# Relative values in a bank of the transposes' ring, and all values of a tile in one run, two steps behind its scores

## What is computed

```python
scores = einsum('bhqd,bhkd->bhqk', Q, K) / SCALE
rel_k = pek[idx]                       # idx = clip(k - q, -256, 256) + 256
scores = scores + einsum('bhqd,qkd->bhqk', Q, rel_k) / SCALE
attn = softmax(where(causal, scores, -inf), axis=-1)
out = einsum('bhqk,bhkd->bhqd', attn, V)
rel_v = pev[idx]
out = out + einsum('bhqk,qkd->bhqd', attn, rel_v)
```

## Time and profile before

| | |
|---|---|
| median of 3 runs | 5531.92 us (5531.32 to 5532.51) |
| the profiled execution | 5535.59 us |
| its span in the profile | 5533.9 us |
| TensorE busy, share of the span | 93% |
| VectorE, ScalarE, GpSimd | 68%, 62%, 33% |
| DMA queue of SP, share of 16 engines | 77.5% |
| mean granted clock of TensorE | 0.990 |

### The profile page before, as it was taken

The page is one execution under the profiler, slowest core; times in us unless marked ns, Lnnn a source line. Parts: engine busy times, 40 slices in busy tenths (PEclk is TensorE's granted clock), DMA queues, the critical chain, the costliest instruction groups (busy, mean ns, idle before and its releaser), DMA issues. The chain is left out here.

```text
span 5533.9 us, 143122 instructions
## 1 busy us (share of the span) xinstructions
PE 5134.9 (93%) x49460; PEld 3347.5 (60%) x49460; DVE 3774.5 (68%) x8777; ACT 3425.3 (62%) x7512; POOL 1831.3 (33%) x2516
## 2 busy tenths in 40 slices
PE   9986999999999999999999999999999799999999
PEld 5554666666666666666666666666666455665665
DVE  5555777777777777777777777777777455555554
ACT  4445888878778887887877878778787211111111
POOL 3443333333333333333333333333333011111111
PEclk9997999999999999999999999999999899999999
DMA  7888999999999999999999999999999311111110
GB/s 223 254 252 264 329 323 324 332 316 323 321 324 324 325 323 321 324 328 325 322 325 327 322 321 327 316 323 327 324 322 304 99 61 56 50 61 61 61 55 32
DMA packets 654368, 1418.07 MB, mean 256 GB/s; under 512 B 64072, under 2 KB 362544, under 8 KB 641456
## 3 DMA queue, kind: packets, MB, share of 16 engines
q1 hardware_dynamic: 653744, 1409.89, 77.5%
HBM read 737.46 MB, written 672.14 MB: 255 GB/s over the span
## 5 line engine op out<-in xcount | busy, mean ns | idle before, releaser
L809 ACT ACTIVATE a_prob<-a_neg_s,a_neg_max 128x384 f32<-128x384 f32 (+1 forms) x1792 | 1081.1, 603 | 209.1 <-DVE a_neg_max L858 193.2
L524 DVE COPY a_p_t<-a_t_ps 128x512 f32<-128x512 f32 (+3 forms) x1536 | 952.5, 620 | 24.8 <-PE a_t_ps L773 23.9
L773 PE MATMUL a_t_ps<-a_ident,a_prob 128*128 128x128 f32 x5120 | 924.5, 280 | 31.5 <-DVE a_p_t L524 20.4
L858 DVE CUSTOM_DVE_ANT_1 a_neg_s<-a_s_ps,a_bias,a_far_neg 128x384 f32<-128x384 f32 x1280 | 791.0, 618 | 237.6 <-DVE a_far_neg L852 237.6
L706 PE MATMUL a_s_ps<-a_k,a_q 96*128 96x512 bf16 (+3 forms) x3072 | 852.7, 332 | 107.2 <-ACT a_far L813 105.1
L852 DVE TENSOR_REDUCE a_far_neg<-a_s_ps 128x1 f32<-128x640 f32 (+4 forms) x1280 | 708.8, 554 | 312.0 <-PE a_s_ps L706 178.5
L816 ACT ACTIVATE a_b_out<-a_t_ps 128x512 f32<-128x512 f32 (+1 forms) x1024 | 587.4, 574 | 384.4 <-PE a_t_ps L716 364.6
L734 PE MATMUL a_o_ps<-a_p_t,a_v 128*32 128x128 f32 x18432 | 782.0, 279 | 7.8 <-ACT a_o_t L821 0.2
L813 ACT ACTIVATE a_far<-a_s_ps,a_neg_max 128x640 f32<-128x640 f32 (+4 forms) x1280 | 730.6, 571 | 0.0
L816 ACT ACTIVATE a_p_t<-a_t_ps 128x512 f32<-128x512 f32 (+3 forms) x1536 | 672.8, 438 | 71.0 <-PE a_t_ps L773 53.4
L773 PE MATMUL a_t_ps<-a_ident,a_far 128*128 128x128 f32 x3840 | 662.5, 278 | 55.5 <-DVE a_p_t L524 52.2
(11 more groups left out here) (99 smaller groups left out, 6678.4 us busy)
## 6 DMA issues: line engine op xcount, KB each, us to landing
a_bias<-bias_scr SPq DMA_DIRECT2D x448, 576.0 KB, 7.8
prob_scr<-a_prob SPq DMA_DIRECT2D x448, 576.0 KB, 6.5
bias_scr<-a_b_out SPq DMA_DIRECT2D x448, 512.0 KB, 7.1
a_band<-prob_scr SPq DMA_DIRECT2D x448, 512.0 KB, 5.6
qk_scr<-p_parts SPq DMA_DIRECT2D x256, 192.0 KB, 3.4
v_scr<-p_v_out SPq DMA_DIRECT2D x256, 128.0 KB, 2.2
a_v<-v_scr SPq DMA_DIRECT2D x64, 512.0 KB, 8.9
attn_scr<-a_o_t SPq DMA_DIRECT2D x512, 64.0 KB, 7.4
```

Of the source, the lines that this page charges most:

```text
L524: copy(p_t[par][:, head, blocks[0] * P:(blocks[-1] + 1) * P], bank[:, 0:len(blocks) * P]) \
L773: mm = pe.transpose(bank[:, n * P:(n + 1) * P], prob_block(r, kk, head, b), ident[:, :])
L809: e = act.activation(near_prob(r, k, u, near(qb)), neg_s[:, u % 2, 0:w].rearrange("p (b c) -> p b c", c=P), ACT.Exp, bias=neg_max[:, u:u + ...
L858: dve.tensor_tensor_reduce(by_block(neg_s[:, u % 2, 0:w]), by_block(s_ps[:, u % 2, lo:lo + w]), near_bias(r, k, u, near(qb)), -1.0, begin, ...
```

## The change

- `P_LAG` goes from 7 to 5: heads are transposed two slots earlier.
- The values of tile k - 2 run in slot 3 of step k, all key blocks in one run, ahead of the slot's ring jobs; before it were those of tile k - 3 in three parts. Their product is closed in `o_ps` by itself.
- The relative values of tile k - 4 become a ring job "rel", the first of slot 3, so that they follow the values directly on TensorE. They go to a bank of the ring.
- ScalarE copies `o_ps` to one of four (before two) slots of `o_t` at the end of slot 3. VectorE adds the ring bank onto it in slot 3 of the step in which "rel" is made, and signals `o_sum`; TensorE waits for `o_sum` before it reuses the bank, SP before it stores.
- With that, an even step has 8 ring jobs and an odd one 14. Of a long tile's four heads, the banks of three are now made in the short tile's step; it was one.

```diff
-        P_LAG = 7
+        P_LAG = 5
         BAND_SLOTS = ((2, 3), (3, 3))
-        VALUE_SLOTS = ((1, 3), (2, 3), (3, 3))
-        REL_SLOT = (0, 4)
+        OUTPUT_SLOT = 3
...
             for u in range(GRP):
+                if u == OUTPUT_SLOT and ok(k - 4) and k >= 0:
+                    jobs.append(("rel", u, k - 4, 0, None))
                 jobs += [("bias", u, kb, c, None) for at, kb, c in bias_jobs(k) if at == u and ok(kb)]
...
             kind, _, kk, i, head = job
-            if kind == "band":
+            if kind == "rel":
+                eng.wait_ge(o_sum, TILES * r + kk + 1)
+            elif kind == "band":
                 eng.wait_ge(r_evac[i], TILES * r + kk + 1)
...
+                if kind == "rel" and name == "dve":
+                    eng.wait_ge(o_mm, TILES * r + kk + 1)
+                    eng.wait_ge(o_evac, TILES * r + kk + 1)
+                    eng.tensor_tensor(o_t[:, kk % OUT], o_t[:, kk % OUT], bank[:, 0:P], ALU.add).then_inc(o_sum, 1)
...
-                        sp.wait_ge(o_evac, T - 3)
+                        sp.wait_ge(o_sum, T - 3)
                         row = attn[r_prev if k < 4 else r]
-                        sp.dma_start(row[g, :, qb * P:(qb + 1) * P], o_t[:, par]).then_inc(stored[par], 16)
+                        sp.dma_start(row[g, :, qb * P:(qb + 1) * P], o_t[:, (k - 4) % OUT]).then_inc(stored[par], 16)
...
-                for j in range((qb + 1) * part // n, (qb + 1) * (part + 1) // n):
+                for j in range(qb + 1):
                     for h in range(GRP):
                         mm = pe.matmul(o_ps[h * VW:(h + 1) * VW, 0:P], v_s[:, g, j, h],
-                                       p_t[par][:, h, j * P:(j + 1) * P], start=(j == 0), stop=False)
...
+                                       p_t[par][:, h, j * P:(j + 1) * P], start=(j == 0), stop=(j == qb))
+                mm.then_inc(pv_mm, 1)
...
                     for h in range(GRP):
-                        mm = pe.matmul(o_ps[h * VW:(h + 1) * VW, 0:P], pv[:, n], band_t[:, par, h, n * P:(n + 1) * P],
-                                       start=False, stop=(n == 1))
+                        mm = pe.matmul(bank[h * VW:(h + 1) * VW, 0:P], pv[:, n], band_t[:, par, h, n * P:(n + 1) * P],
+                                       start=(n == n_first), stop=(n == 1))
...
-                        at, back = VALUE_SLOTS[-1]
-                        if u == at and ok(k - back) and k >= 0:
-                            values(r, k - back, len(VALUE_SLOTS) - 1, first, last)
+                        if u == OUTPUT_SLOT and ok(k - 2) and k >= 0:
+                            values(r, k - 2, first, last)
...
+                            elif kind == "rel":
+                                relative(r, kk, bank)
...
-                        if u == REL_SLOT[0] and ok(k - 4) and k >= 0:
-                            act.wait_ge(o_mm, T - 3)
+                        if u == OUTPUT_SLOT and ok(k - 2) and k >= 0:
+                            act.wait_ge(pv_mm, T - 1)
                             if ok(k - 6):
                                 act.wait_ge(stored[k % 2], pair(r, k - 6))
-                            act.activation(o_t[:, k % 2], o_ps[:, 0:P], ACT.Copy).then_inc(o_evac, 1)
+                            act.activation(o_t[:, (k - 2) % OUT], o_ps[:, 0:P], ACT.Copy).then_inc(o_evac, 1)
```

More of the change, by code:

```diff
@@ L281, in attention @@
     DEPTH = 5
+    OUT = 4
     BIAS_SLOTS = 8
@@ L323, in attention @@
         band_t = sb("a_band_t", [P, 2, GRP, MAXD])
-        o_t = sb("a_o_t", [P, 2, P])
+        o_t = sb("a_o_t", [P, OUT, P])
         s_ps = ps("a_s_ps", [P, 2, seq])
@@ L342, in attention @@
         pv_mm, o_mm, o_evac = sem("a_pv_mm"), sem("a_o_mm"), sem("a_o_evac")
+        o_sum = sem("a_o_sum")
         stored = sem2("a_stored")
         block = ctx.enter_context(nc.Block())
-        P_LAG = 7
+        P_LAG = 5
         BAND_SLOTS = ((2, 3), (3, 3))
-        VALUE_SLOTS = ((1, 3), (2, 3), (3, 3))
-        REL_SLOT = (0, 4)
+        OUTPUT_SLOT = 3
         LOADS = ((0, 0), (0, 1), (0, 2)), ((1, 0), (1, 1)), ((1, 2),)
@@ L719, in biases, with values, relative @@
                 mm.then_inc(b_mm, 1)
-            def values(r, k, part, first, last):
+            def values(r, k, first, last):
                 g, qb, par = (k // QB) % 2, q_block(k), k % 2
[L724 to L731, removed]
-                for j in range((qb + 1) * part // n, (qb + 1) * (part + 1) // n):
+                for name in ("act", "dve"):
+                    pe.wait_ge(t_evac[name], t_done(name, r, k, 0, -1))
+                if k % QB == 0:
+                    pe.wait_ge(v_loaded[g], 16 * (r + k // TILES + 1))
+                if valid(k - 1, first, last):
+                    pe.wait_ge(o_evac, TILES * r + k)
+                for j in range(qb + 1):
                     for h in range(GRP):
                         mm = pe.matmul(o_ps[h * VW:(h + 1) * VW, 0:P], v_s[:, g, j, h],
-                                       p_t[par][:, h, j * P:(j + 1) * P], start=(j == 0), stop=False)
-                if part == n - 1:
-                    mm.then_inc(pv_mm, 1)
-            def relative(r, k):
+                                       p_t[par][:, h, j * P:(j + 1) * P], start=(j == 0), stop=(j == qb))
+                mm.then_inc(pv_mm, 1)
+            def relative(r, k, bank):
                 par = k % 2
@@ L743, in relative @@
                     pe.wait_ge(r_evac[i], TILES * r + k + 1)
-                for n in range(first_j(q_block(k)) // P, 2):
+                n_first = first_j(q_block(k)) // P
+                for n in range(n_first, 2):
                     for h in range(GRP):
-                        mm = pe.matmul(o_ps[h * VW:(h + 1) * VW, 0:P], pv[:, n], band_t[:, par, h, n * P:(n + 1) * P],
-                                       start=False, stop=(n == 1))
+                        mm = pe.matmul(bank[h * VW:(h + 1) * VW, 0:P], pv[:, n], band_t[:, par, h, n * P:(n + 1) * P],
+                                       start=(n == n_first), stop=(n == 1))
                 mm.then_inc(o_mm, 1)
```

## The result

| | before | changed |
|---|---|---|
| median of 4 runs | 5531.62 us | 5970.85 us (5967.54 to 5977.28) |
| profiled execution, its span | as shown above | 5973.27, 5971.5 us |
| mean granted clock | 0.990 | 0.980 |

The ratio is 1.0796, with a 95% interval from 1.0779 to 1.0813: slower by 439 us. The forecast was 6044 us, +512.

The account below looks back on a forecast made before the run. No engine alone bounds it; waits inside a step do. Slot 3 grows by 8 us and the rest frees nothing: 68.4 against 60.4 us a cycle, x 64 = +512, so 6044 us, range 5700 to 6150.

Parts of the forecast that it names:

- The length of the run: TensorE's run of 32-column matmuls: 0.30 us fixed plus 0.028 per instruction, so 2.54 us for 80 instructions.
- The rest of the steps: Step time outside slot 3's stretch up to the second scores: 43.0 us a cycle, against 42.9 before.
- The ring waits: TensorE waits for banks: band.0 for b_out, 3.5 us over four short tiles, and p2 for rel's bank, 1.5 us a cycle.
- the short tile that I worked: Tile 3 (block 2): second scores at 3.3 us, next tile's first scores at 8.6 us, against 7.33 before.
- The block-5 tile: Tile 4, the worked long tile: second scores at 3.35 us, its loop adding 5.4, sum 8.8 us against 8.70 before.
- The add: VectorE's added 128 columns per tile: 0.22 us taken, bounds 0 and 0.68, nearest profiled operation 289 ns.
- The drains: Fixed cost of TensorE's 32-column runs: 21 fewer a cycle at 0.30 us, 6.3 us a cycle, 403 us of its work.
- Rival 1: Ring waits don't bind, as evacuations run early enough: 63.4 us a cycle, 5724 us; chance 0.2.
- Rival 2: VectorE's and ScalarE's backlog covers slot 3's run, if ScalarE idles there under 0.5 us: 59.0 us a cycle, 5442 us; chance 0.12.
- Rival 3: TensorE sets the pace, so the whole 403 us come back: 5129 us; chance 0.02.
- Rival 4: DMA latency of the save and band load loop paces both kernels: both take 5532 us; chance 0.04.
- What would show it: Signs in the changed profile: TensorE busy about 0.7, one run per tile, b_out waits over 0.5 us, DMA about 285 GB/s.

Follow-up runs that it names:

- the four pieces: The changed kernel with VectorE's add split into four pieces of 32 columns instead of one of 128: 6037.3 us, ratio 1.0909.
- the values in parts: The changed kernel with the values of tile k - 2 in three parts in slots 1, 2 and 3 again: 5757.8 us, ratio 1.0408.
- the 16 columns: The changed kernel with values in three parts and VectorE's add over only 16 of 128 columns: 5736.0 us, ratio 1.0364.

## Why the prediction was right, and where its sizes were off

**The direction and the mechanism.** The forecast rested on one sentence: work taken from slots 0 to 2 frees nothing, and slot 3 grows. Slot 3 was to go to 25.4 us a cycle and went to 13.2 + 12.0 = 25.2, tile by tile 2.8 to 3.5 where I had 2.6 to 3.5; the slots before it gave back 1.4 us of the 8.3 and not 0. The 17.5 that I gave for before counts from matmul to matmul; from weight load to weight load, as here, it is 16.9. The run at the end of slot 1 shows that the place costs: same instructions, 187 us less, some 29 of them through the clock, which the forecast didn't have.

**The length of the run** (0.30 + 0.028 for each instruction) held: 64 instructions, 0.126 + 64 x 0.028 = 1.92 us from its start to the next weight load; the trace has 1.89.

**The rest of the steps** is the term that was mis-sized. I had 43.0 us, it is 41.9: 1.1 x 64 = 70 us, nearly all of the 73 by which the forecast was too high. Steps from the first scores of a tile to those of the next, means of the 48 cycles:

| | short, blocks 3, 2, 1, 0 | sum | long, blocks 7, 6, 5, 4 | sum |
|---|---|---|---|---|
| forecast | 8.3, 8.6, 8.0, 7.4 | 32.3 | 9.6, 9.4, 8.8, 8.3 | 36.1 |
| measured | 8.6, 8.4, 7.9, 7.2 | 32.1 | 9.3, 9.2, 8.5, 8.0 | 35.0 |

The excess is in the long tiles, 0.2 to 0.3 us each. The block-5 tile is the one that I worked: behind slot 3 I had 8.8 - 3.35 = 5.45 us for its loop of scores, maximum and exponential, and it is 8.48 - 3.25 = 5.23. Which link of that loop is shorter was not separated.

**The ring waits.** I priced the four waits of band.0 for b_out at 3.5 us a cycle, but the short tile that I worked has only 0.35 for its one (from 7.8 to 7.5 + 0.65), and the trace has 0.33, 1.3 us a cycle. The 3.5 has no working behind it. Nor is it true that no such wait was there before: band.1 waited 0.8 us a cycle for b_out (42.8 us in 3200, 160 times). What I didn't see is that the bias of slot 2 waits too, 1.5 us a cycle; all ring waits for b_out together went from 1.0 to 3.8. The other wait, for the add, I had at 1.5 us in the sum, and it is 73.5 us in 3200, or 47.7 cycles: 1.5.

**The add** is 285 ns, where I had 289 from the nearest row. That its cost reaches the time is shown by the four pieces (+66 us, some 15 of them the clock). With the values in parts the 16 columns bring 22 us of the 58 that I gave to the shortening; whether the absence of the run hides the rest, these two don't tell, since one lengthens the add and the other shortens it.

**The drains.** TensorE's weight-load idle time ended by "issue" fell as forecast: before, the scores' wait 203.9 us and the values' 194.3, with two smaller ones (62.4 and 42.2) 503 us in 53.2 cycles, 9.5 us a cycle; after, 73.7, 45.6 and 38.0 us, 3.3 a cycle. 6.2 us went, against 6.3 expected, and none of it came back as time. TensorE's busy share, which I said would fall to 0.7, is 664 / 800 = 0.83: per cycle it is 55.7 us, 56.2 before. I had taken the drains for a part of that bar. Why the bar stayed as long isn't settled; matmul ends are modelled in it.

**Rival 1** (ring waits don't bind, 5724) is not the case: the waits are there and rel's place alone is worth up to 74 us. It had part of the truth: band.0's wait for b_out is under half of its price. **Rival 2** (backlog covers the run, 5442) fails on its own condition: ScalarE is idle for 1.53 us in the slot shown, not under 0.5. Yet it is nearly what happens in the kernel before with one run (+0.5%): ScalarE waits as long for the transposed bands there as without the run (120.1 us in 3200, 122.3 before; 319.4 in the changed kernel). That fits a backlog which covers the run, but wasn't tested. **Rival 3** (TensorE is the bound) fails in both kernels: 5971 us against its 5129, and +32 us for the one run in the kernel before, which takes 13 runs a cycle away. The Trainium skill (TensorEngine Tiling, Key Properties) says a change of mode drains TensorE; the idle weight loads agree, but as a gain in time no run here shows it. **Rival 4** fails: the cycle grew with the DMA share falling from 0.97 to 0.89.

**What would show it:** one joint run per tile, band copies waited for, jobs waiting for the add, a DMA rate of 290 GB/s (285 said) and no waits for the masked bias all came. Waits of bands for b_out over 0.5 us per short tile didn't: 71.9 / (4 x 47.7) = 0.38. And TensorE's busy share fell to 0.83, not to 0.7.

**How the 439 us divide:** 213 go with the run in slot 3 (5971 to 5758), 74 with the place in the ring (5758 to 5683). That holds in this order only, since the ring place brought 14 with the run still there, and the 213 hold up to 29 of the clock. The last 150 lie in the remaining edits: the add that stays, five slots instead of seven, values at k - 2, and with these the uneven job lists (8 and 14). Shortening the add showed 22 of them. The rest wasn't separated; values in parts at k - 3 with `P_LAG = 7` and rel still in the ring would do it, and was not tried. No kernel here beat the kernel before.

## What to carry to other kernels

Ask of every position in an in-order stream what stands between two links of the loop that sets the pace. In the changed kernel the same block of work costs 187 us more between the first and second scores than two slots earlier; in the kernel before, a run in that place cost 32 us. An idle time that is saved on an engine is worth something only if the next wait on it doesn't simply grow, and moving a piece out of the suspected place is a cheap test of that. When a wait goes into a sum, take it from the tile that was worked: there it was right (0.35 us, measured 0.33), and the price that was not worked was off by more than two. And before two kernels are compared by their times, compare their granted clocks.

## What the runs showed of the hardware that I had not expected

TensorE's granted clock falls when the run is placed last in slot 3, though TensorE's busy share is no lower than in the changed kernel. From 600 to 4200 us, in the changed kernel:

```profile
600.00:4200.00 3600.00, 2987.50 (x37137) 2096.59 (x37135) 2581.58 (x6654) 2545.03 (x5795) 1237.19 (x1450) 0.98 0.89 290
```

and with the run last:

```profile
600.00:4200.00 3600.00, 2995.30 (x36859) 2203.92 (x36857) 2539.40 (x6603) 2581.27 (x5752) 1237.93 (x1437) 0.94 0.89 288
```

The mean of 0.94 is a mixture of the two levels, 2.4 and 1.2 GHz. TensorE is busy 2995 and 2988 us and its weight loads 5% longer for 0.7% fewer instructions. The kernel before has 1.00 in its stage.

What the lower level costs shows in the joint run of 56 instructions (values of the block-4 tile, ahead of the second scores of the block-3 tile). The changed kernel has it at both levels. From its start to the next weight load it takes 2006.40 - 2004.73 = 1.67 us, and one cycle later 2074.50 - 2071.36 = 3.14 us:

```profile
2004.73 1.03 PEld L741 LDWEIGHTS a_o_ps<-a_p_t,a_v 128*32 128x32 f32 x40 [0.23 <-ACT a_p_t L819]
2005.74 0.46 PEld L753 LDWEIGHTS a_t_ps<-a_band_t,a_pv 128*32 128x32 f32 x16
2006.40 0.14 PEld L779 LDWEIGHTS a_t_ps<-a_ident,a_wide 128*128 128x128 f32 x1 [0.20 <-issue]
...
2071.36 1.91 PEld L741 LDWEIGHTS a_o_ps<-a_p_t,a_v 128*32 128x32 f32 x40 [0.44 <-ACT a_p_t L819]
2073.28 0.84 PEld L753 LDWEIGHTS a_t_ps<-a_band_t,a_pv 128*32 128x32 f32 x16
2074.50 0.18 PEld L779 LDWEIGHTS a_t_ps<-a_ident,a_wide 128*128 128x128 f32 x1 [0.38 <-issue]
```

The granted clock of these two stretches (columns as in the earlier trace rows) is 1.00 and 0.50:

```profile
2004.73:2006.40 1.67, 1.67 (x57) 1.47 (x57) 1.40 (x4) 1.30 (x2) 0.11 (x1) 1.00 1.12 346
2071.36:2074.50 3.14, 3.14 (x57) 2.58 (x56) 1.38 (x4) 1.29 (x2) 1.53 (x2) 0.50 1.08 246
```

Over the 48 cycles, with the mean length of that run, and what all joint runs took over their length at 2.4 GHz:

| | falls to 1.2 GHz | us at 1.2 GHz | run of 56, us | joint runs over 2.4 GHz, us in 64 cycles |
|---|---|---|---|---|
| before | 0 | 0 | | |
| changed | 22 | 102 | 1.99 | 29 |
| relative product beside the values | 45 | 181 | 2.60 | 60 |
| run last in slot 3 | 88 | 406 | 2.75 | 118 |
| run at the end of slot 1 | 1 | 3 | | 0 |

The last column is an estimate of what the clock costs, worked out from the lengths of the runs, which stand between first and second scores. Most falls come in one place: in the changed kernel 16 of 22 lie between the third scores of the block-7 tile and the first of the block-3 tile, with the run last 48 of 88 behind its fourth scores. Ahead of them, from the block-7 tile's second scores to the block-3 tile's first, TensorE was busy for 3.54 of 6.03 us in the changed kernel and 3.22 of 5.87 with the run last; it was 5.20 of 6.38 in the kernel before and 4.48 of 6.03 with the run at the end of slot 1, where the clock fell never and once. I read it so: values taken out of the slots in which TensorE waits for exponentials leave it idler there, and the long run behind them pays for that. No kernel here changed the idle time alone.
